# A gated cross-attention and mixture-of-experts block: TensorE tells of its work 8 times a tile in place of 13

## The reference

```python
qp = layernorm(x) @ Wq.T;  kp = rope(ctx @ Wk.T);  vp = rope(ctx @ Wv.T)     # 16 heads of 8
weights = softmax(q @ k.T / sqrt(8));  attn = (weights @ v) @ Wp.T + bp
x = x + tanh(g_xattn) * attn
logits = layernorm(x) @ gate;  the 2 best of 8 experts, softmax over their logits
x = x + tanh(g_ffn) * sum over both: w_e * ((silu(z @ w0_e) * (z @ w1_e)) @ wo_e)
```

## Time and profile before

| | |
|---|---|
| three runs, median | 549.89 us |
| profiled execution, span from first to last instruction | 665.6 us |
| TensorE busy in it | 561.5 us, 84% |
| ScalarE, VectorE, GpSimd busy | 431.8, 393.9, 384.0 us |
| attention, first steady step to the last products | 12.5 to 384.7 us of the span |
| experts | 384.7 to 646.0 us |
| rest, waiting for transfers | 646.0 to 665.6 us |

### The profile page before, as it was taken

How to read it: one execution, slowest core, us unless ns; L and a number is a source line. 1 busy time by engine, 2 the same in 40 slices (tenths; PEclk the granted TensorE clock), 3 DMA queues, 4 the chain that set the end, 5 groups by cost and what they waited for, 6 DMA issues and landing times.

```text
span 665.6 us, 21070 instructions
## 1 busy us (share of the span) xinstructions
PE 561.5 (84%) x6123; PEld 468.0 (70%) x6124; DVE 393.9 (59%) x1418; ACT 431.8 (65%) x1090; POOL 384.0 (58%) x524
## 2 busy tenths in 40 slices
PE   8998898998989899899898779787778978888960
PEld 6886676776767677677776668676677868877860
DVE  6797787777778677677778643372133323223663
ACT  4897787887787788788777735344244546556540
POOL 3347756576575666657566466575545555545651
PEclk9999999999999999999999899897899999999995
DMA  3801111111111111111112112233222222225996
GB/s 91 240 20 57 42 42 52 36 55 40 48 44 36 56 40 48 48 33 58 41 55 63 33 50 73 64 98 101 85 64 80 77 74 76 76 68 174 270 272 206
DMA packets 64242, 52.98 MB, mean 80 GB/s; under 512 B 8607, under 2 KB 60064, under 8 KB 64176
## 3 DMA queue, kind: packets, MB, share of 16 engines
q1 hardware_dynamic: 46560, 30.79, 16.5%
q0 software_dynamic: 8448, 16.93, 7.7%
q10 hardware_dynamic: 9168, 4.46, 2.3%
HBM read 29.44 MB, written 23.22 MB: 79 GB/s over the span
## 4 chain that ended last, share of the span: by engine, by line
PE 51%; another core or an unknown queue 15%; issue 10%; ACT 8%; DVE 6%; ACTq 3%; DMA 2%; DVEq 2%; POOL 1%; SPq 1%; POOLq 0%
PE psK L583 10%; PE psH L603 8%; PE psH L483 5%; PE psH L489 4%; PE psG L498 4%; PE psH L498 3%; PE psK L471 3%; ACT wcur L757 3%; PE psO L619 2%; ACTq L319 2%; ACT ys L771 2%; PE psK L619 2%; ACT hs L764 2%; PE psO L518 2%
## 5 line engine op out<-in xcount | busy, mean ns | idle before, releaser
L1251 POOL DMA_INDIRECT results<-ys,zin x136 | 136.1, 1001 | 106.5 <-ACT ys L771 68.3
L603 PE MATMUL psH<-zT,wcur 128*128 128x128 f32 (+1 forms) x760 | 139.1, 333 | 20.1 <-ACT wcur L757 15.2
L1178 POOL DMA_INDIRECT lists<-zp,dest x128 | 129.6, 1012 | 34.8 <-issue 31.1
L603 PEld LDWEIGHTS psH<-zT,wcur 128*128 128x128 f32 x760 | 112.8, 195 | 34.4 <-ACT wcur L757 20.1
L1083 DVE TENSOR_TENSOR hm<-psH,hs 128x512 f32<-128x512 f32 x68 | 47.0, 692 | 121.0 <-remote 45.7
L977 DVE TENSOR_REDUCE mx<-psH 128x8 fp32r<-128x512 f32 x128 | 82.5, 686 | 43.4 <-PE psH L483 23.6
L696 ACT ACTIVATE ex<-psH,rs 128x512 f32<-128x512 f32 x128 | 86.8, 688 | 23.9 <-PE psH L489 16.3
L583 PEld LDWEIGHTS psK<-v,pT 128*64 128x64 f32 x2048 | 69.6, 137 | 37.1 <-issue 36.3
L583 PE MATMUL psK<-v,pT 128*64 128x64 f32 x2048 | 81.1, 226 | 9.0 <-issue 8.6
L757 ACT COPY wcur<-w 128x512 f32 x95 | 56.1, 619 | 15.2 <-issue 14.2
L747 ACT COPY v<-kvr 64x64 f32<-64x64 f32 x256 | 63.7, 249 | 2.2
(11 more groups left out here) (176 smaller groups left out, 1140.5 us busy)
## 6 DMA issues: line engine op xcount, KB each, us to landing
yy<-results SPq DMA_DIRECT2D x16, 512.0 KB
zin<-lists SPq DMA_DIRECT2D x41, 130.0 KB
out_dram<-x ACTq DMA_DIRECT2D x16, 256.0 KB
xring<-in_x_dram SPq DMA_DIRECT2D x31, 128.0 KB
cring<-in_ctx_dram SPq DMA_DIRECT2D x31, 128.0 KB
zin<-lists SPq DMA_DIRECT2D x54, 65.0 KB
results<-ys,zin POOLq DMA_INDIRECT x136
w<-in_L_ffn_w_kernel_dram SPq DMA_DIRECT2D x2, 1024.0 KB, 7.1
```

What stands on the lines that cost most here:

```text
L603: last = pe.matmul(bank[t.buf(2)][:, k * ET + c.start:k * ET + c.stop], wcur[:, t.buf(2), h, a, k * P:(k + 1) * P], zT[:, t.buf(2), c], st ...
L1178: nc.gpsimd.indirect_dma_start(lists, bass.IndirectOffsetOnAxis(ap=dest[:, t.buf(4), j:j + 1], axis=0), zp[:, t.buf(4), j, :], None).then_ ...
L1251: nc.gpsimd.indirect_dma_start(results, bass.IndirectOffsetOnAxis(ap=zin[:, t.buf(8), h, D:D + 1].bitcast(U32), axis=0), ys[:, t.buf(8), h ...
```

## The change

Where two of TensorE's updates stand side by side, the first is left out and its waiters wait for the second, which now tells of both. No instruction changes its place on any engine. The five merges:

- L583 of a step is told with L465 of the next step (`xc_pv`)
- L518 with the second `shift` (`shift1_attn`)
- L471 with L541 (`kv_oT`)
- the turns of L498 into psG with L476 (`q_p1`)
- the scores of heads 8 to 15 with those of heads 0 to 7 (`s_ps`)

The waiters count accordingly: x1 of tile t waits until the shift of tile t+2 has been counted, and so on. In the last steps, where the partner is absent, the first keeps its update. VectorE's second maximum no longer waits for the scores by itself, since the first one has.

```diff
+        def inputs_are_turned(eng, t, back=0):
+            wait_for(eng, xc_pv, t, back=back)
+        def attention_there(eng, t, back=0):
+            wait_for(eng, xc_pv, t + 4, back=back)
+        def second_shifted(eng, t):
+            wait_for(eng, shift1_attn, t)
+        def output_there(eng, t, back=0):
+            wait_for(eng, shift1_attn, t + 2, back=back)
+        def keys_values_there(eng, t):
+            wait_for(eng, kv_oT, t)
+        def output_is_turned(eng, t, back=0):
+            wait_for(eng, kv_oT, t + 4, back=back)
+        def queries_there(eng, t):
+            wait_for(eng, q_p1, t)
+        def second_are_turned(eng, t, back=0):
+            wait_for(eng, q_p1, t + 2, back=back)
...
-                    pe.matmul(psK[:, 0:2 * D], ..., wT[:, 1:3, :], ...).then_inc(kv_ps, 1)
+                    last = pe.matmul(psK[:, 0:2 * D], ..., wT[:, 1:3, :], ...)
+                    if signal:
+                        last.then_inc(kv_oT, 1)
...
-                    pe.matmul(psO[:, 0:P], wT[:, 0, :], ...).then_inc(q_ps, 1)
+                    pe.matmul(psO[:, 0:P], wT[:, 0, :], ...).then_inc(q_p1, 1)
...
-                        last.then_inc(s_ps[h], 1)
+                        if h == 0:
+                            last.then_inc(s_ps, 1)
...
-                        last.then_inc(shift_ps[h], 1)
+                        last.then_inc(shift1_attn if h else shift0_ps, 1)
...
-                        last.then_inc(p_ps[h], 1)
+                        if signal:
+                            last.then_inc(q_p1 if h else p0_ps, 1)
...
-                        pe.matmul(psO[:, 368:368 + XW], oT[:, t.buf(2), :], wTg[:, :], ...).then_inc(attn_ps, 1)
+                        last = pe.matmul(psO[:, 368:368 + XW], oT[:, t.buf(2), :], wTg[:, :], ...)
+                        if not ATT_PE.at(s, 2):
+                            last.then_inc(shift1_attn, 1)
...
-                        keys_values(t)
+                        keys_values(t, signal=not ATT_PE.at(s, 1))
...
-                        turn(t, 1)
+                        turn(t, 1, signal=not ATT_PE.at(s, 4))
...
-                        last.then_inc(pv_ps, 1)
+                        if not ATT_PE.at(s, 6):
+                            last.then_inc(xc_pv, 1)
...
                     if t := ATT_DVE.at(s, 0):
-                        wait_for(dve, attn_ps, t)
+                        output_there(dve, t)
...
                     if t := ATT_ACT.at(s, -2):
-                        wait_for(act, p_ps[1], t)
-                        wait_for(act, pv_ps, t, back=2)
+                        second_are_turned(act, t)
+                        attention_there(act, t, back=2)
                         probabilities(t, 1)
```

More of the change, by code:

```diff
@@ L213, in flamingo_block @@
         st1_done, mv1_done, ve_done, rs_done, nm_done = sem("st1_done"), sem("mv1_done"), sem("ve_done"), sem("rs_done"), sem("nm_done")
-        xc_ps, xc_sb = sem("xc_ps"), sem("xc_sb")
-        q_ps, kv_ps, q_sb, rope_done = sem("q_ps"), sem("kv_ps"), sem("q_sb"), sem("rope_done")
+        xc_pv, xc_sb = sem("xc_pv"), sem("xc_sb")
+        q_p1, kv_oT, q_sb, rope_done = sem("q_p1"), sem("kv_oT"), sem("q_sb"), sem("rope_done")
         v9_done, kT_ps, k_sb = sem("v9_done"), sem("kT_ps"), sem("k_sb")
[L217 to L221, removed]
+        s_ps, mx_done = sem("s_ps"), [sem(f"mx_done{h}") for h in range(2)]
+        shift0_ps, shift1_attn, exp_done = sem("shift0_ps"), sem("shift1_attn"), [sem(f"exp_done{h}") for h in range(2)]
+        p0_ps, p_sb = sem("p0_ps"), [sem(f"p_sb{h}") for h in range(2)]
+        rden_done, on_done = sem("rden_done"), sem("on_done")
+        oT_sb, x1_done, logit_done = sem("oT_sb"), sem("x1_done"), sem("logit_done")
         st2_done, mv2_done, wq_step, gate_ps, gate_ready, wo_ready = sem("st2_done"), sem("mv2_done"), sem("wq_step"), sem("gate_ps"), sem("gate_ready"), sem("wo_ready")
@@ L339, in load_ready @@
                     carry(sp)
-                    wait_for(sp, xc_ps, t + 1, back=4)
+                    inputs_are_turned(sp, t + 1, back=4)
                     wait_for(sp, st1_done, t + 1, back=4)
@@ L464, in inputs_turned, with keys_values @@
                     pe.transpose(psX[:, 0:P], xring[:, t.buf(4), :], ident[:, :])
-                    pe.transpose(psX[:, P:2 * P], cring[:, t.buf(4), :], ident[:, :]).then_inc(xc_ps, 1)
-                def keys_values(t):
+                    pe.transpose(psX[:, P:2 * P], cring[:, t.buf(4), :], ident[:, :]).then_inc(xc_pv, 1)
+                def keys_values(t, signal=True):
                     wait_for(pe, xc_sb, t)
@@ L470, in keys_values @@
                     wait_for(pe, on_done, t, back=4)
-                    pe.matmul(psK[:, 0:2 * D], xcT[:, t.buf(8), P:2 * P], wT[:, 1:3, :], start=True, stop=True).then_inc(kv_ps, 1)
+                    last = pe.matmul(psK[:, 0:2 * D], xcT[:, t.buf(8), P:2 * P], wT[:, 1:3, :], start=True, stop=True)
+                    if signal:
+                        last.then_inc(kv_oT, 1)
                 def queries(t):
@@ L475, in queries @@
                     wait_for(pe, oT_sb, t, back=3)
-                    pe.matmul(psO[:, 0:P], wT[:, 0, :], xcT[:, t.buf(8), 0:P], start=True, stop=True).then_inc(q_ps, 1)
+                    pe.matmul(psO[:, 0:P], wT[:, 0, :], xcT[:, t.buf(8), 0:P], start=True, stop=True).then_inc(q_p1, 1)
                 def attention_step(s):
@@ L491, in shift, with turn @@
                                              start=False, stop=True, skip_group_check=True)
-                        last.then_inc(shift_ps[h], 1)
-                    def turn(t, h):
+                        last.then_inc(shift1_attn if h else shift0_ps, 1)
+                    def turn(t, h, signal=True):
                         for n in range(4):
@@ L517, in attention_step @@
                         pe.matmul(psO[:, 368:368 + XW], xcT[:, t.buf(8), 0:P], idg[:, :], start=True, stop=False, skip_group_check=True)
-                        pe.matmul(psO[:, 368:368 + XW], oT[:, t.buf(2), :], wTg[:, :], start=False, stop=True, skip_group_check=True).then_inc(attn_ps, 1)
+                        last = pe.matmul(psO[:, 368:368 + XW], oT[:, t.buf(2), :], wTg[:, :], start=False, stop=True, skip_group_check=True)
+                        if not ATT_PE.at(s, 2):
+                            last.then_inc(shift1_attn, 1)
                     if t := ATT_PE.at(s, 2):
@@ L540, in attention_step @@
                         wait_for(pe, x1_done, t, back=1)
-                        pe.transpose(psO[:, P:2 * P], on[:, t.buf(2), :], ident[:, :]).then_inc(oT_ps, 1)
+                        pe.transpose(psO[:, P:2 * P], on[:, t.buf(2), :], ident[:, :]).then_inc(kv_oT, 1)
                     if t := ATT_PE.at(s, 2):
@@ L706, in attention_step @@
                     if t := ATT_ACT.at(s, 1):
-                        wait_for(act, xc_ps, t)
-                        wait_for(act, attn_ps, t, back=8)
+                        inputs_are_turned(act, t)
+                        output_there(act, t, back=8)
                         nc.scalar.copy(xcT[:, t.buf(8), :], psX[:, 0:2 * P]).then_inc(xc_sb, 1)
                     if t := ATT_ACT.at(s, -2):
-                        wait_for(act, shift_ps[0], t)
-                        wait_for(act, p_ps[0], t, back=2)
+                        wait_for(act, shift0_ps, t)
+                        wait_for(act, p0_ps, t, back=2)
                         wait_for(act, rs_done, t + (0 if t.buf(2) else 1))
@@ L715, in attention_step @@
                     if t := ATT_ACT.at(s, -2):
-                        wait_for(act, shift_ps[1], t)
-                        wait_for(act, p_ps[1], t, back=2)
+                        second_shifted(act, t)
+                        second_are_turned(act, t, back=2)
                         wait_for(act, rs_done, t + (0 if t.buf(2) else 1))
@@ L720, in attention_step @@
                     if t := ATT_ACT.at(s, -3):
-                        wait_for(act, oT_ps, t)
-                        wait_for(act, attn_ps, t, back=2)
+                        output_is_turned(act, t)
+                        output_there(act, t, back=2)
                         nc.scalar.copy(oT[:, t.buf(2), :], psO[:, P:2 * P]).then_inc(oT_sb, 1)
@@ L726, in attention_step @@
                     if t := ATT_ACT.at(s, -2):
-                        wait_for(act, p_ps[0], t)
-                        wait_for(act, pv_ps, t, back=2)
+                        wait_for(act, p0_ps, t)
+                        attention_there(act, t, back=2)
                         probabilities(t, 0)
                     if t := ATT_ACT.at(s, -2):
-                        wait_for(act, p_ps[1], t)
-                        wait_for(act, pv_ps, t, back=2)
+                        second_are_turned(act, t)
+                        attention_there(act, t, back=2)
                         probabilities(t, 1)
                     if t := ATT_ACT.at(s, 0):
```

(22 more changed lines are left out.)

## The result

The changed kernel takes 571.43 us (median of 4 runs, 570.58 to 572.15), the kernel before 549.94 (4 runs beside it, 549.31 to 550.67): ratio 1.0388, 95% interval 1.0365 to 1.0411, 21.5 us slower. The forecast was 566, with a range of 550 to 572: the direction and the mechanism held, the size was 5.5 us short.

What follows compares the result with a forecast made beforehand. TensorE's serial chain was taken to bound attention, about 4.8 us a step. Two later signals add 0.31 us a step, 14 to 19 us in all; the middle, 16 us, on 549.9 gives 566 us, range 550 to 572.

Steps and rivals of the forecast that it cites:

- TensorE's chain sets the pace of attention: In a clean attention step the chain of waits is TensorE from end to end; the step takes 4.81 us.
- late updates: TensorE's signals arriving long after their instruction, waits of about 1.5 us in attention; at most 28 us fit into a run.
- the middle: Total cost in attention taken as 16 us, between 14 us with 18 disturbed steps and 19 us with all clean.
- The bound: Run time less experts, start and tail leaves attention at most 321 us, 5.26 us for each of 61 steps.
- Merge 1: L518 told with the second shift: x1 and then L541 come later, 0.17 us a step.
- the slack: Delay absorbed between x1 and L541's matmul: 0.20 us lag less 0.15 where TensorE truly waited, 0.05 us.
- Merge 2: Turns of L498 into psG told with L476: the copy L701, then products L583, come later, 0.14 us a step on average.
- Merges 3 to 5: L583 told with next L465, L471 with L541, the scores' two halves together: each hidden, cost 0.
- the updates themselves: A semaphore update takes nothing visible from TensorE's issue: at most 0.01 us each, 3 us in all, taken as 0.
- They add: The delays of L518's signal and the psG turns' signal lie in one serial chain and sum to 0.31 us a step.
- The marks in the profile: Signs expected afterwards: L1003 and L701 start later, L541 0.15 behind L1004, early attention steps lengthen from 4.8 to 5.1 us.
- Rival C: Faster: fewer TensorE updates held up during GpSimd's scatters ahead of L1003, near 547 us, or 533; chance 0.12.

Runs made afterwards that it cites:

- experiment 6: The kernel before with L518 told by the first of the second shift's two matmuls, 13 updates a tile: 555.05 us, ratio 1.0096.
- experiment 3: The change without the merges of L518 and of the turns into psG, 10 updates a tile, against the kernel before: 550.61 us, ratio 1.0011.
- experiment 4: The kernel before with five more TensorE updates a tile that nobody waits for, 18 a tile: 550.44 us, ratio 1.0005.
- experiment 7: The kernel before with only the merges of L518 and of the turns into psG, 11 updates a tile: 572.41 us, ratio 1.0397.
- experiment 5: The kernel before, unedited, profiled a second time: 549.99 us in one run, span 548.2 us.

## Why the prediction was right, and where its size was off

- **TensorE's chain sets the pace of attention.** Right: the step of the second profile before is 4.81 us, and 20.6 of the 20.8 us between the spans lie in attention.
- **The runs hardly have late updates** (at most 5.26 us a step). Right, and more so than I used it: the second profile, whose run took 549.99 us, has none that shows. The mis-sized term is the middle that I took between 14 us (18 disturbed steps) and 19 us (all clean). All clean was the right one; that is 3 of the missing 5.5 us. The bound itself pointed there, had I counted right: the stretch from 12.5 us to the last products holds all 64 groups of L583, so 64 steps and not 61, the last three without L464. That makes 321 / 64 = 5.0 us a step, and at most about 64 x 0.2 = 13 us of late updates, not 28. (The profiled execution's average is 5.8 us, not 6.1.)
- **Merge 1, 0.22 - 0.05 = 0.17 us a step, 62 steps, 10.5 us.** Mechanism right, size 11.7 us measured. The second mis-sized term is the slack: 0.05 us in the step of the earlier trace rows and the other written-out ones, none in the 40 steps of the loop. That is another 1.2 us by the runs (2 by the steps' lengths); experiment 6 points the same way. The last 1.3 us of the 5.5 are within what the measurements tell.
- **Merge 2, 0.14 us a step, 9 us.** 9.0 us measured (interval 7.6 to 10.3). The terms hold as well: 0.13 us ahead of the products in most steps, 0.19 in every fourth, where I had 0.22. The slack, 0.15 - 0.11, was taken from a wait of another instruction with two semaphores, and L617's weight load does follow by 0.11 to 0.12 once it truly waits.
- **Merges 3 to 5 and the updates themselves, 0.** Right within what the runs can tell (experiments 3 and 4); the trace of experiment 3 shows 0.12 us in one step of eight.
- **They add.** Right (experiment 7). 11.7 + 9.0 = 20.7 of 21.5 us; the remaining 0.8 is less than the measurement tells.
- **The marks in the profile.** L1038 behind the shift, L575 0.15 behind x1, L736 behind the queries, L617's load 0.12 behind L736, early steps of 5.1 us: each is there. The gap from L471 to L541 grew by 0.17 (0.43 to 0.60) in the early steps, and by 0.22 in the loop.
- **Rival C** rested on the late updates being in the runs; experiments 3, 4 and 5 show runs without them, and three updates fewer saved nothing.

No experiment points to a version that beats the kernel before: the three harmless merges give nothing that can be measured.

## What to carry to other kernels

A semaphore update that nobody is late for cost nothing here, but one moved behind 0.22 us of further work cost 0.13 to 0.22 us at every step, because its waiter had next to nothing else to do and the waiter's result goes back to the engine that sets the pace. Before merging two signals, find for each waiter the idle time ahead of it and the lag between its result and the instruction that needs it, compared with the lag where that instruction truly waited; read it in the loop, not in the written-out steps. And when a profile's span is far over the runs' time, bound what the runs can contain, and profile again before reading waits from it.

## What the runs showed that was not expected

- One execution of the kernel before spanned 665.6 us against 548.2 of the next, with 14 waits of L1003 for updates that came over 1.5 us late; every other profile here has a span within 3 us of the median of its runs.
- 320 further semaphore updates by TensorE cost 1.3 us at most.
- The first weight load of the products follows the end of the copy that it waits for by 0.11 to 0.12 us when it truly waits, and the matmul of L541 follows x1 by 0.15.
- The lag between x1 and L541 is not the same in the written-out steps (0.20 us) and in the loop (0.15), though the work is the same. Why L1004 follows L1003 a little later in the loop stays open.
